# Issuing GpSimd's product of B two steps ahead, in front of the expert's product

## The reference

```python
h = layernorm(x) * (1 + ca) + sa
x = x + ga * mamba_both(h)          # layernorm again, then a forward and a backward Mamba, plus its input
h = layernorm(x) * (1 + cb) + sb
x = x + gb * moe(h)                 # 8 experts, top 2 chosen per position, plus one shared expert
# one Mamba direction, 256 inner channels, 16 states:
u, z = split(x @ Win.T); u = silu(conv4(u)); dtr, B, C = split(u @ Wx.T)
dt = softplus(dtr @ Wdt.T + bdt)
h[n] = exp(dt * A[n]) * h[n] + (dt * u) * B[n]      # over the 512 positions
y = sum_n h[n] * C[n] + u * D;  out = (y * silu(z)) @ Wout.T
# one expert: (hh * sigmoid(hh) * (x @ w2)) @ w3 with hh = x @ w1
```

## Time and profile before

| | |
|---|---|
| median of three runs | 2608.17 us (2607.06 to 2610.25) |
| profiled execution | 2608.1 us, span 2606.3 us, granted TensorE clock 0.903 |
| busy: VectorE, TensorE, GpSimd, ScalarE | 2288.7, 2115.5, 1957.9, 1510.3 us |
| a body with all parts | some 155 us, of which there are 14 |

### The profile page before, as it was taken

The page is one execution under the profiler, slowest core; times in us unless marked ns, Lnnn a source line. Parts: engine busy times, 40 slices in busy tenths (PEclk is TensorE's granted clock), DMA queues, the critical chain, the costliest instruction groups (busy, mean ns, idle before and its releaser), DMA issues. The chain is left out here.

```text
span 2606.3 us, 37957 instructions
## 1 busy us (share of the span) xinstructions
PE 2115.5 (81%) x9893; PEld 1352.7 (52%) x9893; DVE 2288.7 (88%) x3603; ACT 1510.3 (58%) x2468; POOL 1957.9 (75%) x1437
## 2 busy tenths in 40 slices
PE   3677887878788797888879788797978879798868
PEld 1244554545555455555546555454555545555554
DVE  1699998989899898998989899899989989899973
ACT  2546656655565665656666555665556566565633
POOL 1577878778787877878777787877878787787854
PEclk8777998989899898998989899898989989899989
DMA  2334233333323333332333323233332333333310
GB/s 82 129 130 138 102 131 106 110 127 113 130 98 128 108 114 122 113 125 103 114 124 115 135 97 130 106 109 127 113 130 97 128 108 114 122 113 124 114 67 5
DMA packets 120494, 293.33 MB, mean 113 GB/s; under 512 B 18516, under 2 KB 53172, under 8 KB 120388
## 3 DMA queue, kind: packets, MB, share of 16 engines
q1 hardware_dynamic: 120388, 292.30, 32.8%
HBM read 285.91 MB, written 6.34 MB: 112 GB/s over the span
## 5 line engine op out<-in xcount | busy, mean ns | idle before, releaser
L426 POOL TENSOR_TENSOR bt<-v,bb 128x1024 f32<-128x1024 f32 x512 | 1207.1, 2361 | 176.5 <-DVE psA L787 173.7
L787 DVE TENSOR_TENSOR_SCAN psA<-psA,bt 128x512 f32<-128x512 f32 x1024 | 1199.4, 1218 | 114.4 <-POOL bt L426 91.6
L600 ACT ACTIVATE psA<-dt,aneg 128x512 f32<-128x512 f32 x1024 | 688.1, 688 | 821.0 <-DVE g L797 816.3
L987 PEld LDWEIGHTS psY<-ident,g 128*128 128x128 f32 x4096 | 519.4, 152 | 474.7 <-DVE g L797 262.3
L987 PE MATMUL psY<-ident,g 128*128 128x128 f32 x4096 | 608.6, 295 | 160.9 <-DVE g L797 160.7
L797 DVE TENSOR_TENSOR g<-psA,cb 128x512 f32<-128x512 f32 x1024 | 676.0, 680 | 0.0
L526 POOL TENSOR_TENSOR act<-pf,gf 128x512 f32<-128x512 f32 x288 | 366.2, 1272 | 252.1 <-DVE pf L882 220.9
L1068 PE MATMUL F<-h2T,w 128*128 128x512 f32 x576 | 334.2, 664 | 92.9 <-DVE pf L882 92.9
L1112 PE MATMUL F<-w,act 128*128 128x128 f32 x2304 | 318.6, 283 | 43.7 <-POOL act L526 41.7
L1112 PEld LDWEIGHTS F<-w,act 128*128 128x128 f32 x2304 | 291.4, 198 | 60.9 <-issue 53.9
L1071 PE MATMUL F<-h2T,w 128*128 128x512 f32 x576 | 308.9, 619 | 0.0
(11 more groups left out here) (133 smaller groups left out, 1724.6 us busy)
## 6 DMA issues: line engine op xcount, KB each, us to landing
bb<-bc_rows SPq DMA_DIRECT2D x256, 512.0 KB, 3.6
cb<-bc_rows SPq DMA_DIRECT2D x256, 512.0 KB, 3.6
x<-in_L_attn_x SPq DMA_DIRECT2D x16, 256.0 KB, 3.8
xR<-in_L_attn_x SPq DMA_DIRECT2D x16, 256.0 KB, 3.6
out_x<-osb SPq DMA_DIRECT2D x16, 256.0 KB, 3.9
w<-in_L_ffn_ew SPq DMA_DIRECT2D x2, 1024.0 KB
modA<-mod_table SPq DMA_DIRECT2D x16, 128.0 KB, 3.9
bc_rows<-xd SPq DMA_DIRECT2D x32, 64.0 KB, 3.0
```

The source lines that it names most:

```text
L426: g.tensor_tensor(bt[:, n % 2, :, :], v[d][:, :, :], bb[:, n // 2 % 2, n % 2, :].unsqueeze(1).broadcast_to([P, NH, T]), ALU.mult).then_inc ...
L600: s.activation(psA[:, half * T:half * T + T], dt_[d][:, half, :], ACT.Exp, scale=aneg[d][:, half, n:n + 1]).then_inc(a_s, 1)
L787: w.tensor_tensor_scan(ah, ah, bt[:, n % 2, half, :][:, order], 0.0, ALU.mult, ALU.add)\
L987: last = m.matmul(psY[:, half * T + i * P:half * T + i * P + P], g_[:, n % 2, half, i * P:i * P + P], ident[:, :], is_transpose=True, star ...
```

## The change

`bmul` is called two steps ahead instead of one, and stays first in GpSimd's list of the slot. As `bt` has two buffers, the product of step s+2 waits for the scans of step s, those of its own slot. Two products are made ahead of the first body. `make_v` moves one slot earlier, behind `make_dt` in slots 10 and 29, since the first product of a direction is now due in slots 14 and 30. Only GpSimd's list changes.

```diff
@@ -531,28 +531,29 @@
                     norms(prep_f, slot)
                     if slot == PREP_SLOT[0] + DT_AT + 3:
                         make_dt(prep_f, 0)
-                    if slot == PREP_SLOT[0] + V_AT:
+                    if slot == PREP_SLOT[0] + V_AT - 1:
                         make_v(prep_f, 0)
                 if prep_b and slot == PREP_SLOT[1] + DT_AT + 3:
                     make_dt(b, 1)
-                if prep_b and slot == PREP_SLOT[1] + V_AT:
+                if prep_b and slot == PREP_SLOT[1] + V_AT - 1:
                     make_v(b, 1)
 
             for slot in range(STEPS):
                 side(-1, slot, False, 0, False)
             bmul.unit = 1
             bmul(0, 0, 0)
+            bmul(1, 0, 1)
 
             def body(b, scan, ffn, last):
                 for slot in range(STEPS):
                     if scan:
-                        nxt = slot + 1
+                        nxt = slot + 2
                         if nxt < STEPS:
                             bmul.unit = 2 * b + 1 + nxt // N
                             bmul(STEPS * b + nxt, nxt // N, nxt % N)
                         elif not last:
                             bmul.unit = 2 * b + 3
-                            bmul(STEPS * b + nxt, 0, 0)
+                            bmul(STEPS * b + nxt, 0, nxt - STEPS)
                     if slot == 0 and not (isinstance(b, int) and b < 2):
                         output(b - 2)
                     if scan:
```

## The result

The changed kernel takes 2622.07 us in the median of 4 runs (2619.17 to 2625.32) against 2607.98 us before on the same chip: a ratio of 1.0052, 95% interval 1.0037 to 1.0067, 14 us slower. The forecast was 2611 in a range of 2590 to 2632. The profiled execution is the longest of these four, 2625.3 us with a span of 2623.5.

A forecast was written before the change was run, and what follows sets the result against it. VectorE was taken as the engine to fill, waiting for bt made late by GpSimd's queue order. 14 samples x 0.11, -1.4 for the last sample and +3 for half clock gave +3 us on 2608.17: 2611, range 2590 to 2632.

The forecast's parts named there:

- The bound: VectorE's scans wait for bt, late by GpSimd's queue order: 5.72 us in one body, 80 of 91.6 over 14 samples.
- Slots 5 to 10: Of 2.82 us of waits removed in slots 7 and 8, ScalarE's queue leaves 1.37, by which the scan of slot 10 comes earlier.
- Slots 10 to 16: GpSimd's dense stretch ends 0.87 us late, delaying slot 16's down product; the scan of slot 18 moves +0.11 a sample.
- +0.11 for the up product of slot 16: TensorE's up product in slot 16 starts at 1067.67 instead of 1067.56, behind the late down product.
- The clock: Half clock after slot 16's longer gap on TensorE in 2 of 14 samples at 1.6 us: +3 us.
- nearly always in slot 14, where A(5) covers it and fills slot 16's gap: Half clock was expected behind slot 14's 3.4 us gap, hidden by GpSimd's expert product, leaving TensorE less idle before slot 16.
- Rival 2: Slower: half clock in slot 16's longer gap in every sample, 1.6 us each, 22 us in all, 2631; chance 0.15.
- The last sample: With no next sample to prepare, its GpSimd queue is loose and keeps what it wins in slots 7 and 8: -1.4 us.
- The signs named in advance: If right: no bt waits in slots 7, 8, 14 to 16, act waits of 6 or 7 us a sample, period within 0.4.
- rival 2's sign: Granted clock of a half just after the down product of slot 16, named as showing the forecast wrong.

The follow-up runs named there:

- e2: The kernel before with the products two ahead in slots 5 to 9 only, dt and v where they were: 2589.39 us, 0.9927 of before.
- e9: The changed kernel with 2, 3 and 2 extra unread matmuls in TensorE's gaps of slots 12, 14 and 16, except in the last two bodies: 2604.55 us, 0.9980 of before.
- e3: The kernel before with the products two ahead in slots 10 to 17 only and backward v in slot 10: 2648.46 us, 1.0145 of before.

## Why the forecast was right in its range and low in its size

**The bound.** Right: GpSimd's order, not its work, made bt late, and the waits for it in slots 7, 8 and 14 to 16 went as said (77 us of the 91.6, where 80 were counted from one body).

**Slots 5 to 10.** Right: ScalarE's queue was next. Scan(10) came 1.5 earlier in bodies 6 and 13, where 1.37 was worked out, and e2 shows that this gain is real and survives when act keeps its place.

**Slots 10 to 16.** Right in mechanism, off in small terms. bt(12) to A(5) took 35.55, worked out 35.67; A(5) ended 0.62 later within body 13 than before, worked out 0.87; the up product started 0.44 after the transposes, not 0.60. Together they turn +0.11 for the up product of slot 16 into -0.31 in body 13, and scan(18) came 0.40 earlier there. In e9, where no half clock falls from slot 12 to 18, bodies 1 to 14 take 6.2 us less than before: the faster side of the forecast, 0.9980.

**The clock.** This term was mis-sized, and it carries the result: +3 us forecast (2 of 14 samples at 1.6), 19 to 23 measured. The step that failed is "nearly always in slot 14, where A(5) covers it and fills slot 16's gap". The change opened three gaps, and I asked only of two of them what follows. Behind slot 14's gap half clock fell in 1 body of 14 and not nearly always, and so slot 16's gap stayed at 2.7 in 13 of 14. The gap in slot 12 (2.31) was the first to bring half clock, in 9 bodies, around the up products of its slot; that left 1.7 to 1.9 of slot 14's gap and TensorE on time, and bare, in slot 16. It need not fall in slot 12 first: with slots 12 and 14 filled (e11) half clock still came behind slot 16's gap in 7 of 14 bodies. Rival 2 named the mechanism, its place and its price (1.6 a sample, 2631 if it strikes every sample); it struck in 9 of 14. In the profiled executions half clock adds 23.2 and the order takes 6.2 in bodies 1 to 14; body 0 adds 2.1, the start takes 0.7 and body 15 with what follows 1.3. These make the 17 between the spans. That 2622 lies within the range is no merit of the sum, which put this term at 3: the range reached far enough towards rival 2, which had been given 0.15.

The Trainium skill's rule ("TensorE: Matmul & The Clock Gate", The HAM clock gate) that the array falls to 1.2 GHz after idling was named in the prediction as the risk of each longer gap. The runs agree: the same order of GpSimd's queue is 1.0052 of before with the gaps and 0.9980 with the gaps filled.

**What was left out.** Body 0 lost 2.1 us: most of its slots up to there are 3.75 to 4.0 us long, and scan(13) waited for a bt that stood behind the moments, dt and v. The row of the changed kernel:

```profile
139.71 2.34 DVE L788 TENSOR_TENSOR_SCAN psA<-psA,bt 128x512 f32<-128x512 f32 x2 [2.12 <-POOL bt L426]
```

The last sample won 2.7 us by its slot 31 (139.14 after its first scan, before 141.85), forecast 1.4; the expert part of body 16 then lost 1.4.

**The signs named in advance.** No wait for bt in slots 7, 8 and 14 to 16, ScalarE's release of scan(9), no gap up to A(5), waits for act of 6 to 7 us a sample (6.8 in body 6, 8.5 in body 13, without half clock) and new waits for tf, facc and gate_y all came. The period did not stay within 0.4: 156.02 in body 6, before 154.96. Half clock behind slot 16's down product, named as rival 2's sign, is what was seen.

## What to carry to other kernels

An in-order queue whose list is full for tens of microseconds has only an order to give away: moving one product ahead makes all that stands behind it later by its length, so ask whose consumer has no slack, and move it only in the slots where the queue idles (here that was 0.7% faster, the whole move 0.5% slower). When a change opens gaps on TensorE, list every new gap and ask of each what runs right behind it; in front of a stretch in which TensorE was full (slots 16 to 18) the half clock behind a gap could not be made good. To learn whether it is the late product or the half clock that costs, fill the gap with matmuls that nobody reads, and only in the bodies that have the gap.

## What the runs showed of the hardware

With the gaps of slots 12 and 14 filled (e11), slot 16's gap was 2.81 us in body 8 and the matmuls behind it ran at full clock:

```profile
1385.06 1.13 PE L1116 MATMUL F<-w,act 128*128 128x128 f32 x8 [2.81 <-POOL act L526]
1386.03 0.60 PE L1042 MATMUL psP<-ident,xn 128*128 128x128 f32 x4
1386.46 1.02 PE L1069 MATMUL F<-h2T,w 128*128 128x512 f32 x2
```

In body 9 and every second body around it (5 to 13) half clock did follow a gap of 2.8, and the periods of bodies 6 to 13 alternate between 154.6 and 156.0. In the changed kernel bodies 8 to 11 all take 157.0 to 157.2 with half clock at the same place, in e3 nearly all bodies 156.7 to 157.4. So whether a gap of this length brings half clock depends on more than its length, and the loop can settle into a period in which it does each time. Single executions of the changed kernel lie 6 us apart (2619.17 to 2625.32); this may be why, but it is not shown. What sets it was not tried.
